# A graph network on one core: sixteen ranges per register load, root products in two halves, and a scale chain moved behind attention tiles

## The reference

```python
def _sage(x, src, dst, W_l, b_l, W_r):                 # layer 0, run for both directions of the edges
    msg_sum = segment_sum(x[src], dst, num_segments=N_NODES)
    cnt = segment_sum(ones, dst, num_segments=N_NODES)
    aggr = msg_sum / maximum(cnt, 1.0)[:, None]
    return aggr @ W_l.T + b_l + x @ W_r.T              # x @ W_r.T are the "root products"

# layer 1: linear attention: per head instance_norm of k and v, dots = k^T v / N, out = q dots w_out
# layer 1: a second graph layer with W_l, W_r, gamma, beta; the kernel keeps its sums in fp16 with a scale
#          worked out from the largest row length of W_l, of gamma and of beta
```

## Time and profile before

| | before |
|---|---|
| median of 3 runs | 1829.48 us |
| profiled execution | 1833.38 us |
| its span, first to last instruction | 1831.6 us |
| TensorE busy | 1674.0 us (91%) |
| VectorE busy | 966.3 us (53%) |
| ScalarE busy | 669.4 us (37%) |
| GpSimd busy | 235.8 us (13%) |
| mean granted TensorE clock | 0.961 |

### The profile page before, as it was taken

How to read it: one execution, slowest core, us unless ns; L and a number is a source line. 1 busy time by engine, 2 the same in 40 slices (tenths; PEclk the granted TensorE clock), 3 DMA queues, 4 the chain that set the end, 5 groups by cost and what they waited for, 6 DMA issues and landing times. The chain is left out here.

```text
span 1831.6 us, 31389 instructions
## 1 busy us (share of the span) xinstructions
PE 1674.0 (91%) x9423; PEld 1104.4 (60%) x9424; DVE 966.3 (53%) x2821; ACT 669.4 (37%) x1352; POOL 235.8 (13%) x290
## 2 busy tenths in 40 slices
PE   6889888987979899999799899999997989998998
PEld 5344555665747423333656799999955557644657
DVE  7888889887568664244511100000055874345862
ACT  3112444674024576665121344444321432201220
POOL 2100000001010003900044000000065000500002
PEclk8999999999989999999599999999998999999989
DMA  2000121225750000000513312211121002141001
GB/s 85 0 15 29 59 87 67 107 116 194 236 155 7 1 1 1 1 1 1 188 58 115 132 66 90 84 63 66 63 84 34 1 1 82 58 145 42 1 1 60
DMA packets 86409, 118.86 MB, mean 65 GB/s; under 512 B 6789, under 2 KB 72511, under 8 KB 86177
## 3 DMA queue, kind: packets, MB, share of 16 engines
q1 hardware_dynamic: 80992, 106.53, 17.2%
q0 software_dynamic: 3936, 10.37, 1.8%
q10 hardware_dynamic: 1376, 0.66, 0.1%
HBM read 70.66 MB, written 46.87 MB: 64 GB/s over the span
## 5 line engine op out<-in xcount | busy, mean ns | idle before, releaser
L804 PE MATMUL bank<-onehot_key,onehot_low 128*128 128x320 bf16 x1304 | 223.4, 303 | 38.2 <-DVE onehot_low L603 23.8
L599 DVE TENSOR_SCALAR onehot_key<-iota_keys,edge_keys 128x640 bf16<-128x640 f16 x652 | 231.5, 381 | 27.5 <-PE bank L804 22.7
L804 PEld LDWEIGHTS bank<-onehot_key,onehot_low 128*128 128x128 bf16 x1304 | 104.3, 99 | 147.9 <-DVE onehot_key L599 55.0
L2647 ACT ACTIVATE hidden<-bank,b_cols 128x128 f32<-128x128 f32 x344 | 126.4, 367 | 178.2 <-PE bank L2574 154.7
L2728 DVE TENSOR_TENSOR slot_columns<-bank,b_rows 128x256 f32 x43 | 18.3, 425 | 290.3 <-PE bank L2580 290.3
L2574 PEld LDWEIGHTS bank<-slot_columns,w 128*128 128x128 f32 x1376 | 162.8, 194 | 5.6 <-issue 3.4
L2574 PE MATMUL bank<-slot_columns,w 128*128 x1376 | 163.2, 278 | 3.2 <-issue 3.2
L2580 PE MATMUL bank<-w,hidden 128*128 128x256 f32 x688 | 155.6, 379 | 0.0
L671 ACT ACTIVATE edge_low_shifted<-edge_low,window_offset 128x631 f32 x81 | 66.7, 823 | 192.1 <-DVE onehot_low L603 191.2
L2580 PEld LDWEIGHTS bank<-w,hidden 128*128 128x128 f32 x688 | 127.4, 190 | 15.5
L1739 ACT ACTIVATE XT<-bank 128x512 f32<-128x512 f32 x160 | 84.3, 603 | 57.8 <-PE bank L1667 57.8
(11 more groups left out here) (517 smaller groups left out, 2745.4 us busy)
## 6 DMA issues: line engine op xcount, KB each, us to landing
AT_dram<-at_strip SPq DMA_DIRECT2D x20, 640.0 KB, 4.0
A_dram<-a_strips SPq DMA_DIRECT2D x20, 640.0 KB, 2.9
sg_strip<-AT_dram SPq DMA_DIRECT2D x20, 640.0 KB, 4.0
back_strip<-A_dram SPq DMA_DIRECT2D x24, 480.0 KB, 5.0
w<-in_L_ffn_W1p SPq DMA_DIRECT2D x8, 1024.0 KB, 5.3
w<-in_L_ffn_W2p SPq DMA_DIRECT2D x8, 1024.0 KB, 7.8
slot_rows<-ty_zero SPq DMA_DIRECT2D x1, 6144.0 KB, 24.5
slot_columns<-slot_rows SPq DMA_DIRECT2D x12, 512.0 KB, 8.7
```

Source lines behind the costliest of these rows:

```text
L599: dve.tensor_scalar(ohk[:, q, :], ioh[:, :], key[:, ds(chunk(n, offset, q), 1)], None, ALU.is_equal).then_inc(s_key[q], 1)
L804: last = pe.matmul(bank[2 * (x % 2) + h][:, 0:HB], ohl[q // 2][:, :, q % 2], ohk[:, q, h * HB:(h + 1) * HB], start=False, stop=q == Q - 1, ...
L2647: act.activation(hid[:, f, 0:P], bank[f % 4][:, 0:P], ACT.Gelu, bias=b1[:, ds((e + 1) * FB + f, 1)]).then_inc(s_rg, 1)
```

## The change

It does four things.

1. `fetch_tile` becomes `fetch_some`: TensorE and VectorE load FETCH = 16 ranges by one call every 16 windows, instead of XW = 4 every 4. The place of the call within a window is the same.
2. The root products of a tile are made one node tile at a time: the first (four instructions) behind window 1, the second behind window 2. The wait for `s_fc` moves with the first. ScalarE's copy stays in window 3.
3. On TensorE, L2888 moves from behind `kv(1)` to behind `dots(3)`.
4. On ScalarE the two squarings move behind tile 2 and the root behind tile 7. On VectorE the two reductions of gamma and beta move behind tile 4, the maximum of the weights and its clamp behind tile 5, and the other five instructions behind tile 8.

```diff
+            FETCH = 16
+            assert NW % FETCH == 0
-                def fetch_tile(eng, w):
+                def fetch_some(eng, w):
-                    return list(nc.values_load_multi_w_load_instructions(par[0:1, w:w + XW], engines=[eng.engine])[1])
+                    return list(nc.values_load_multi_w_load_instructions(par[0:1, w:w + FETCH], engines=[eng.engine])[1])
...
-                            if w % XW == 0:
-                                loaded.extend(fetch_tile(eng, w + 1))
+                            if w % FETCH == 0:
+                                loaded.extend(fetch_some(eng, w + 1))
...
+                        def root(j, i):
+                            t = 2 * j + i
+                            for c in range(CB):
+                                last = pe.matmul(bank[6 + j % 2][:, i * 2 * P:(i + 1) * 2 * P], XT[:, c, t * P:(t + 1) * P], wr[:, c, :], start=c == 0, stop=c == CB - 1)
+                            if i == 1:
+                                last.then_inc(s_rp, 1)
...
-                            if x == RT and ROOTS + t < ZN:
-                                if t >= 2:
+                            if x in (RT - 1, RT) and ROOTS + t < ZN:
+                                if x < RT and t >= 2:
                                     pe.wait_ge(s_fc, t - 1)
-                                roots(ROOTS + t)
+                                root(ROOTS + t, x - (RT - 1))
...
-                        pe.wait_ge(s_wq, 1)
-                        for c in range(CB):
-                            last = pe.matmul(bank[7][:, 0:C], onesf[:, :], wsq[:, c, :], start=c == 0, stop=c == CB - 1)
-                        last.then_inc(s_wn, 1)
                         for t in range(T):
                             if t + DEEP - 1 < T:
                                 kv(t + DEEP - 1)
                             dots(t)
+                            if t == 3:
+                                pe.wait_ge(s_wq, 1)
+                                for c in range(CB):
+                                    last = pe.matmul(bank[7][:, 0:C], onesf[:, :], wsq[:, c, :], start=c == 0, stop=c == CB - 1)
+                                last.then_inc(s_wn, 1)
...
-                        act.wait_ge(s_sw, 16 * 8)
-                        act.activation(wsq[:, :, :], sg_w[:, :, 0:C], ACT.Square).then_inc(s_wq, 1)
-                        act.activation(gq[:, :, :], sg_gb[:, 0:2, :], ACT.Square).then_inc(s_wq, 1)
-                        act.wait_ge(s_gm, 1)
-                        act.activation(gz[:, 3:6], gz[:, 0:3], ACT.Sqrt).then_inc(s_gr, 1)
...
+                            if t == 2:
+                                act.wait_ge(s_sw, 16 * 8)
+                                act.activation(wsq[:, :, :], sg_w[:, :, 0:C], ACT.Square).then_inc(s_wq, 1)
+                                act.activation(gq[:, :, :], sg_gb[:, 0:2, :], ACT.Square).then_inc(s_wq, 1)
+                            if t == 7:
+                                act.wait_ge(s_gm, 1)
+                                act.activation(gz[:, 3:6], gz[:, 0:3], ACT.Sqrt).then_inc(s_gr, 1)
...
+                            if t == 4:
+                                dve.wait_ge(s_wq, 2)
+                                dve.tensor_reduce(gz[:, 1:2], gq[:, 0, :], AX.X, ALU.max)
+                                dve.tensor_reduce(gz[:, 2:3], gq[:, 1, :], AX.X, ALU.add)
+                            if t == 5:
+                                dve.wait_ge(s_wn, 1)
+                                st.then(dve.tensor_reduce(gz[:, 0:1], bank[7][:, 0:C], AX.X, ALU.max))
+                                dve.tensor_scalar(gz[:, 0:3], gz[:, 0:3], 1e-20, None, ALU.max).then_inc(s_gm, 1)
+                            if t == 8:
+                                dve.wait_ge(s_gr, 1)
...
+                                dve.tensor_scalar(sg_sf[:, :], indeg[:, :], gz[:, 6:7], None, ALU.mult)
+                                dve.tensor_scalar(sg_w[:, :, 0:C], sg_w[:, :, 0:C], gz[:, 7:8], None, ALU.mult)
```

More of the change, by code:

```diff
@@ L759, in roots @@
                             for i in range(2):
-                                t = 2 * j + i
-                                for c in range(CB):
-                                    last = pe.matmul(bank[6 + j % 2][:, i * 2 * P:(i + 1) * 2 * P], XT[:, c, t * P:(t + 1) * P], wr[:, c, :], start=c == 0, stop=c == CB - 1)
-                            last.then_inc(s_rp, 1)
+                                root(j, i)
                         pe.wait_ge(s_gm, 1)
@@ L2963, in _ @@
                         st = Steps(dve, s_ch)
-                        dve.wait_ge(s_wq, 2)
-                        dve.tensor_reduce(gz[:, 1:2], gq[:, 0, :], AX.X, ALU.max)
-                        dve.tensor_reduce(gz[:, 2:3], gq[:, 1, :], AX.X, ALU.add)
-                        dve.wait_ge(s_wn, 1)
-                        st.then(dve.tensor_reduce(gz[:, 0:1], bank[7][:, 0:C], AX.X, ALU.max))
-                        dve.tensor_scalar(gz[:, 0:3], gz[:, 0:3], 1e-20, None, ALU.max).then_inc(s_gm, 1)
-                        dve.wait_ge(s_gr, 1)
-                        st.then(dve.scalar_tensor_tensor(out=gz[:, 6:7], in0=gz[:, 4:5], scalar=float(C) ** 0.5, in1=gz[:, 5:6], op0=ALU.mult, op1=ALU.add))
-                        st.then(dve.scalar_tensor_tensor(out=gz[:, 6:7], in0=gz[:, 6:7], scalar=1.0 / (HALF_SCALE * C ** 0.5), in1=gz[:, 3:4], op0=ALU.mult, op1=ALU.mult))
-                        st.then(dve.reciprocal(gz[:, 7:8], gz[:, 6:7]))
-                        dve.tensor_scalar(sg_sf[:, :], indeg[:, :], gz[:, 6:7], None, ALU.mult)
-                        dve.tensor_scalar(sg_w[:, :, 0:C], sg_w[:, :, 0:C], gz[:, 7:8], None, ALU.mult)
                         for t in range(T):
@@ L2988, in _ @@
                             dve.tensor_tensor(by_head(K[k][:, :]), by_head(bank[KV[t % DEEP][0]][:, :]), spread(ss[k][:, 2, 0:Hh], 2, Dh), ALU.mult).then_inc(s_k, 1)
+                            if t == 4:
[8 more added lines that the diff above has]
+                                dve.wait_ge(s_gr, 1)
+                                st.then(dve.scalar_tensor_tensor(out=gz[:, 6:7], in0=gz[:, 4:5], scalar=float(C) ** 0.5, in1=gz[:, 5:6], op0=ALU.mult, op1=ALU.add))
+                                st.then(dve.scalar_tensor_tensor(out=gz[:, 6:7], in0=gz[:, 6:7], scalar=1.0 / (HALF_SCALE * C ** 0.5), in1=gz[:, 3:4], op0=ALU.mult, op1=ALU.mult))
+                                st.then(dve.reciprocal(gz[:, 7:8], gz[:, 6:7]))
+                                dve.tensor_scalar(sg_sf[:, :], indeg[:, :], gz[:, 6:7], None, ALU.mult)
+                                dve.tensor_scalar(sg_w[:, :, 0:C], sg_w[:, :, 0:C], gz[:, 7:8], None, ALU.mult)
                         dve.wait_ge(s_use, T)
```

## The result

| | before | after |
|---|---|---|
| median, measured side by side (20 runs each) | 1828.95 us | 1836.87 us |
| range of these runs | 1819.93 to 1834.03 | 1829.09 to 1840.75 |
| profiled execution | 1833.38 us | 1831.26 us |
| its span | 1831.6 us | 1829.5 us |
| TensorE busy | 1674.0 us | 1663.4 us |

The ratio is 1.0037, 95% interval [1.0024, 1.005]: **slower by 0.37%, 6.8 us**; the two medians are 7.9 us apart. The forecast was 8.6 us slower, 1838.1 us. The 20 runs of the changed kernel fall into two groups, six of 1829.1 to 1832.2 us with a mean granted clock of 0.960 to 0.962, the profiled one among them, and fourteen of 1835.7 to 1840.8 us with 0.954 to 0.958.

A forecast was written before the change was run, and what follows sets the result against it. Edge stage taken as bound by VectorE and TensorE with one group of lookahead, linear attention by TensorE. Loads and clock +10.5, roots 0, chain -1.9 gave +8.6 us on median 1829.48: 1838.1 us, range 1822 to 1850.

The forecast's parts named there:

- fifteen loads removed: Edge stage: 15 of 20 four-value loads per engine go, 14 at 1.5 us and window 4's at 4.0, saving 25.0 us.
- five larger loads and their clock: Edge stage: five loads of sixteen cost 5.42 us more each, 27.1 us; lowered clock behind four of them adds 8.4 us.
- root products: Edge stage: halves make two waits of 0.86 us for one of 1.73, so 0; bounds +0.6 and -10 us.
- scale chain: Start of linear attention: first dots 2.8 us earlier, L2888 adds 0.9, sum -1.9 us.
- I take the line through the two rows that exist: Loads of sixteen: 217 and 235 ns a value continued from loads of one and four, growing 2.60 and 2.82 us.
- (a): Edge stage loads: sixteen values grow little; 1802.6 us if by nothing, 1823.0 if by 1.2 us per engine; chance 0.17.
- (b): Edge stage: the holes don't bring the clock down, 8.4 us less, +0.2, 1829.7 us; chance 0.12.
- (c): Edge stage: each load is cut into sixteen single loads, 39.5 instead of 27.1, +21.0, 1850.5 us; chance 0.10.
- (e): Edge stage: half a root product does fit somewhere, -8, total +0.6, 1830.1 us; chance 0.05.
- I count the low stretch as staying: Start of linear attention: the low-clock stretch, 2.5 us, was counted as remaining, though no row settled it.
- the -4.4 that the spread named: Start of linear attention: the chain's gain in us if the clock stays up, instead of -1.9.
- (d): Start of linear attention: VectorE gets between GpSimd's additions and clock stays up, -7.3 instead of -1.9; +3.2, 1832.7 us; chance 0.06.

## Why the prediction was nearly right

Step by step, by the two traces; the windows of the edge stage are those between L607/L609 rows.

| step | forecast | measured |
|---|---|---|
| fifteen loads removed | -25.0 | -24.6, all other windows |
| five larger loads and their clock | 27.1 + 8.4 = +35.5 | +39.5, window 0 and the tiles of windows 16, 32, 48, 64 |
| root products | 0 | -0.4, the six pairs of windows |
| scale chain | -1.9 | -4.9 (alone: -3.5) |
| sum | +8.6 | +9.7 (before rounding) |
| medians | +8.6 | +7.9, ratio 1.0037 |

**Loads removed: right.** Windows 20, 24 and 28 are 4.07 to 4.36 us now, 5.61 before. Window 4 takes 7.18 instead of 11.29 us: 4.1 against the 4.0 taken, and its split holds, since with the clock up and the load of four in place it is 9.67 us, 1.6 less.

**Larger loads: the mechanism right, the size short by 4.0 us.** The values cost their 217 and 235 ns in a load of sixteen as in one of four, and the two engines' loads stand one behind the other, with no cover. In window 0, where no transfer runs and the clock fell before too, the cost is 41.39 - 35.96 = 5.43 us against 5.42 forecast; the closeness is in part luck, since in the trace of the loads alone the same window is 40.55 us, 4.6 more than before. The four others cost 8.4, 8.0, 8.5 and 9.1 us (read over the tile of four windows) against 5.42 + 2.1. The missing term is contention: beside the strips' transfers VectorE's loads (5.65, 5.11, 5.07 and 4.46 us) grew over their 3.62 us by 2.0, 1.5, 1.5 and 0.8 us, and TensorE's last by 0.45, together 6.3 us, where my sum has nothing. The step that failed reads "I take the line through the two rows that exist". It took the line also for places where the longer load reaches into a transfer, though the earlier trace rows had the hint: a TensorE load of 1845 ns among nineteen of about 1007. I had put it down as "the longer one" and used it for the clock, and had not asked what was beside it. ScalarE's loads of one value (L362) had the hint too, with a median of 282 ns and up to 875 in the trace of before. At 127 us, within TensorE's long load, that trace has

```profile
127.00:128.00 1.00, 0.00 (x0) 0.00 (x0) 0.70 (x3) 0.00 (x0) 0.00 (x0) 0.58 1.07 445
```

Of the +39.5 us, 27.1 are the values and 6.3 the contention; 6.1 remain for the clock, against 8.4 forecast. The kernel with the loads moved two windows agrees from the other side: there window 18 is 12.09 instead of 4.08 and window 19 6.99 instead of 5.80, together 9.2 us for loads of 7.4, so 1.8 us for the clock against 2.1 taken.

The Trainium skill (SBUF — State Buffer, section SBUF: two separate sides) says that engine ports and DMA ports are disjoint and that a DMA is not slowed by a compute operation nor the other way round. A register load is on neither list; the runs show that it is slowed.

**Rivals (a), (b), (c).** (a) fell: 3.62 us, not under 2.8. (b) fell: the clock fell behind each of the four loads (at 206, 288, 353 and 401 us). (c) fell: five rows, not eighty; and even eighty separate loads of one value are no dearer than twenty of four, since single loads partly hide.

**Roots: right** but for 0.4 us,'s argument as it stands: 1.73 us became 0.86 twice, and with it (e) fell.

**Chain: the hold right, the clock on the other side.** The hold came as worked out: L2977 ends with L2863, the first dots 2.9 us earlier (2.8 forecast), TensorE idle for 2.58 us (3.0). L2899 took its 1.03 us among the matmuls, and the pieces on VectorE and ScalarE stayed under cover (the idle time ahead of L2976 shrinks to 0.22 and 0.18 us in two tiles and to nothing in the one behind the last five instructions, but TensorE never waits again: the dots go on every 4.33 us, and once 5.19 with L2899). What I had left unsettled, "I count the low stretch as staying", went the other way: the clock stayed up, and the -4.4 that the spread named for that case is -4.9 measured. Alone it did fall, for 5 us instead of 8. Both happen, and in both the gain was larger than the 1.9 us forecast, since the low stretch, where there was one, was shorter than before.

**Rival (d)** fell as a result of this change, and its mechanism was then made on purpose: with GpSimd's additions spread, attention is 7.2 us shorter, close to the -7.3 us worked out for VectorE getting in. The Trainium skill (SBUF — State Buffer, section Who interferes with whom) says that the one that issues first holds the shared pair "for the whole instruction", and that a tensor_reduce never contends while a tensor_scalar can. The trace agrees on the second point (L2976, 1.22 us inside GpSimd's row, is not lengthened; L2977 behind it is). On the first it agrees for an addition that stands alone (0.64 instead of 0.17 us in the kernel with the additions spread and the chain in its old place). For a row without gaps it differs: one of GpSimd's additions is 0.69 us, and VectorE stood for 4.68, some seven of them.

So +8.6 was close in part by luck: two sizes were off in opposite directions, 4.0 us too little cost for the loads and 3.0 too little gain for the chain. And the +7.9 of the medians is itself uncertain by some microseconds, by what the clock does in stages that the change doesn't touch.

## What to carry to other kernels

Loading more registers at once doesn't amortise anything once the price is per value: compare the slope of the load against its fixed part, and prefer many short ones that the engine's queued work can cover over one that leaves a hole (here 80 loads of one beat 5 of sixteen by some 22 us). When an instruction is made longer, look at what it will then lie beside, and treat every outlier in the durations of its present form as a sample of that. A row of GpSimd instructions without a gap can hold a small VectorE tensor_scalar from SBUF to SBUF until its end; a wait that ties each to the other engines' progress gave 3 to 4 us of the attention stage here, at the price of one or two holds of half a microsecond.

## What the runs showed of the hardware that I had not expected

- A register load out of SBUF slows down while DMAs move 410 to 445 GB/s: one value 0.30 to 0.9 us, four 1.0 to 1.85 (TensorE), eight 1.95 to 4.0 (TensorE), sixteen 3.62 to 5.65 (VectorE). Moved away, sixteen take 3.61 again.
- A load of one value behind queued matmuls costs TensorE nothing; VectorE pays its 0.3 us in both places of the window that were tried, unless it waits there anyway.
- VectorE's tensor_scalar waited through some seven back-to-back GpSimd additions (4.68 us), not only through the one that ran; a single addition held a tensor_tensor until its own end (0.64 instead of 0.17 us).
- The clock's falls in stages that no edit touches move the time by several us: 326.1 or 318.4 to 320.9 us behind the last dots, 970.8 to 979.9 us ahead of attention. A change worth 4 us can't be judged by the spans of one profile of each kernel.
